# Decoder block on one core: softmax division in the output additions, biases of Wv on ScalarE, first Wo split on two engines, values of head pairs transposed together

## The reference, cut to what matters

```python
# B=4 batches, T=512 rows, C=512 columns
q = x @ Wq + bq;  k = x @ Wk + bk;  v = x @ Wv + bv     # 16 "heads" of 128, x layer-normed
att = softmax(q_T @ k / sqrt(128))                      # 128 x 128 per head: over the channels, not over the rows
x1 = x + (att @ v).reshape(...) @ Wo + bo
# cross attention of x1 (layer-normed) with ctx: 8 heads of 64 channels
x2 = x1 + gamma * softmax(q_h.T @ k_h / 8) @ v_h        # 512 x 512 per head and batch, v = k = ctx
# feed-forward with weights rounded to -s, 0, s
x3 = x2 + (silu(LN(x2) @ w1q.T) * (LN(x2) @ w3q.T)) @ w2q.T
```

## Time and profile before

| | before |
|---|---|
| time, median of 3 runs | 1224.45 us (1220.92 to 1225.1) |
| profiled execution, its own time | 1221.23 us |
| its span, first to last instruction | 1219.4 us |
| PE busy | 1144.5 us, 94% |
| DVE, ACT, POOL busy | 791.8 us (65%), 536.4 us (44%), 461.5 us (38%) |
| chain that ended last | PE 78%, DVE 11%, ACT 4%, POOL 2% |
| TensorE clock granted, mean | 0.983 of full speed |

### The profile page before, as it was taken

One profiled execution on the slowest core, in us unless ns is written; L12 is line 12 of the kernel. 1 busy time (PEld: TensorE's weight loads), 2 busy tenths in 40 slices (PEclk: granted clock), 3 DMA queues, 4 the chain that ended last, 5 costly groups with the idle time before them and its releaser, 6 DMA issues.

```text
span 1219.4 us, 16711 instructions
## 1 busy us (share of the span) xinstructions
PE 1144.5 (94%) x5856; PEld 952.4 (78%) x5856; DVE 791.8 (65%) x1469; ACT 536.4 (44%) x1129; POOL 461.5 (38%) x392
## 2 busy tenths in 40 slices
PE   4999988999999999899999978779999999999998
PEld 3888876878788888788888856568878887888786
DVE  7566559889465666453452378878867886787531
ACT  2455562314041244441232227657727762875230
POOL 2222249041341133461403026446625651674030
PEclk9999989999999999999999979979999999999999
DMA  6465553555302143312200132921103110310000
GB/s 224 131 186 181 185 173 109 180 175 170 110 19 85 59 156 113 127 55 70 69 1 1 35 129 66 323 70 54 52 21 102 51 35 34 94 46 1 35 1 35
DMA packets 50480, 114.76 MB, mean 94 GB/s; under 512 B 9721, under 2 KB 9721, under 8 KB 48362
## 3 DMA queue, kind: packets, MB, share of 16 engines
q1 hardware_dynamic: 50410, 113.84, 29.0%
HBM read 97.03 MB, written 16.79 MB: 93 GB/s over the span
## 4 chain that ended last, share of the span: by engine, by line
PE 78%; DVE 11%; ACT 4%; issue 3%; POOL 2%; DMA 1%; SPq 0%; POOLq 0%; ACTq 0%; DVEq 0%
PE bank L102 15%; PE bank L103 15%; PE bank L104 15%; PE bank L435 6%; PE bank L434 6%; PE bank L398 4%; PE bank L446 3%; PE bank L447 3%; PE bank L408 2%; PE bank L409 2%; PE bank L420 2%; PE bank L421 2%; POOL wal L1400 1%; DVE wlow L1352 1%; DVE wraw L1354 1%
## 5 line engine op out<-in xcount | busy, mean ns | idle before, releaser
L1063 ACT ACTIVATE yh<-bank 128x512 fp32r<-128x512 f32 x64 | 38.3, 598 | 244.4 <-PE bank L104 244.4
L434 PE MATMUL bank<-x3h,w 128*128 128x512 f32 (+1 forms) x352 | 141.4, 402 | 1.6 <-DVE x3l L678 1.6
L758 POOL TENSOR_SCALAR pe_x<-pe_x,xri,gam 128x512 f32<-128x512 f32 x128 | 100.9, 789 | 106.4 <-DVE xri L613 100.6
L435 PE MATMUL bank<-x3l,w 128*128 128x512 f32 (+1 forms) x352 | 138.9, 395 | 0.0
L1400 POOL TENSOR_TENSOR wal<-raw_a,wah 128x512 fp32r<-128x512 f32 x48 | 67.5, 1437 | 175.1 <-ACT wah L1084 175.1
L102 PE MATMUL bank<-yh,rh 128*128 128x512 f32 x256 | 101.5, 396 | 7.1 <-DVE xacc L1287 7.0
L1405 POOL TENSOR_TENSOR wbl<-raw_b,wbh 128x512 fp32r<-128x512 f32 x64 | 95.0, 1517 | 34.2 <-ACT wbh L1095 34.2
L102 PE MATMUL bank<-wah,ph 128*128 128x512 f32 x256 | 101.6, 397 | 6.6 <-POOL wal L1400 6.6
L609 DVE TENSOR_REDUCE xmx<-bank 128x1 f32<-128x512 f32 x128 | 87.4, 683 | 28.0 <-PE bank L409 26.8
L523 ACT ACTIVATE pe_x<-bank,xmx 128x512 f32<-128x512 f32 x128 | 87.9, 686 | 37.7 <-DVE xmx L609 36.3
L102 PE MATMUL bank<-wah,gh 128*128 128x512 f32 x256 | 101.0, 394 | 1.7 <-POOL wal L1400 0.8
(11 more groups left out here) (138 smaller groups left out, 2982.9 us busy)
## 6 DMA issues: line engine op xcount, KB each, us to landing
raw_a<-in_wk SPq DMA_DIRECT2D x8, 1024.0 KB, 5.2
raw_b<-in_wq SPq DMA_DIRECT2D x8, 1024.0 KB, 5.3
raw_a<-in_wo SPq DMA_DIRECT2D x8, 1024.0 KB, 5.8
raw_b<-in_wvt SPq DMA_DIRECT2D x8, 1024.0 KB, 4.8
x1d<-x_scratch SPq DMA_DIRECT2D x64, 128.0 KB, 2.7
kd<-in_ctx SPq DMA_DIRECT2D x64, 128.0 KB, 2.8
ternary_scratch<-wraw SPq DMA_DIRECT2D x24, 341.2 KB, 3.0
w<-ternary_scratch SPq DMA_DIRECT2D x2, 2730.0 KB
```

The lines of the kernel that those rows point to most:

```text
L434: pe.matmul(u_bank[w][0:m, :], lhs, x3h[:, c, :], start=c == 0, stop=False)
L435: mm = pe.matmul(u_bank[w][0:m, :], lhs, x3l[:, c, :], start=False, stop=c == CK - 1)
L758: pool.tensor_scalar(pe_x[:, q, :], pe_x[:, q, :], xri[:, q:q + 1], gam[:], ALU.mult, ALU.mult).then_inc(s["xpn"], 1)
```

## The change

Four edits are made together.

1. The exponentials are transposed undivided. `pe_t` waits for the exponentials (`s_read`), `dve_shares` makes one reciprocal of 128 x 8 sums for a group and keeps it (`rinv` has a place for each group), and `dve_out` multiplies by it while it adds: an operation with two tensors and one number per partition in place of an addition.
2. `dve_bias_v` only makes the four columns `dv`. ACT adds them to `raw_b` in four activations (`vadd`) ahead of its four copies in `act_split_b`. They stand behind ACT's wait for the last products that read `wbh`.
3. The first split of Wo (`step == GROUPS`) is shared as those of Wk are: DVE chunks 0 and 1, POOL chunks 2 and 3. `act_matrix(p, 0)` goes from the end of group 3's tiles into them (after the tiles of chunk 1).
4. The values of two heads are transposed together at `q == 0` of even heads, from a new tile `vd` (128 rows of ctx, one buffer, an added transfer of 256 KB for each pair of heads). ACT and DVE split a pair in one operation of 512 columns each. For odd heads SP no longer waits for a transpose. The tiles in `t_bank` are 40 in a turn, not 44.

```diff
@@ sp_head
             if h >= 2 or not isinstance(b, int) or b > 0:
                 sp.wait_ge(s["ql"], n - 1)
                 gate(sp, "sp")
-                sp.wait_ge(s["t_ready"], t_v(b, h - 2) + 1 if h >= 2 else t_v(b - 1, XH - 2 + h) + 1)
+            if h % 2 == 0:
+                if h or not isinstance(b, int) or b > 0:
+                    sp.wait_ge(s["t_ready"], t_v(b, h - 2) + 1 if h else t_v(b - 1, XH - 2) + 1)
+                sp.dma_start(vd[:], rows(ctx, b)[XD * h:XD * (h + 2), :]).then_inc(s["vd_in"], 16)
@@ pe_vt
-                mm = pe.transpose(tb[:, c * P:(c + 1) * P], kd[:, h % 2, c * P:(c + 1) * P], ident[:])
+                mm = pe.transpose(tb[:, c * P:(c + 1) * P], vd[:, c * P:(c + 1) * P], ident[:])
@@ pe_turn (act_turn and dve_turn alike)
-                        if q == 0:
+                        if q == 0 and h % 2 == 0:
                             pe_vt(pe, b, h)
@@ act_vt, dve_vt
+        def v_tile(h):
+            tb = t_bank[t_v(0, h) % 2][:].rearrange("p (c e n) -> p e c n", e=2, n=XD)
+            return tb, vts[:, h % 4:h % 4 + 2, :, 0:XD], vts[:, h % 4:h % 4 + 2, :, XD:P]
-            act.activation(vts[:, h % 4, :, 0:XD], tb[:, :, 0:XD], ACT.Copy).then_inc(s["vth"], 1)
+            act.activation(high, tb, ACT.Copy).then_inc(s["vth"], 1)
+            dve.tensor_tensor(low, tb, high.bitcast(F32), ALU.subtract).then_inc(s["t_free"], 1)
@@ pe_t
-                pe.wait_ge(s["pn"], n + 1)
+                pe.wait_ge(s["s_read"], n + 1)
@@ act_split_b
+            if step >= GROUPS:
+                act.wait_ge(s["dv"], GROUPS * p + step - GROUPS + 1)
+                for c in range(CK):
+                    act.activation(raw_b[:, c, :], raw_b[:, c, :], ACT.Identity, bias=dv[:, c:c + 1]).then_inc(s["vadd"], 1)
@@ act_scores
-                if g == GROUPS - 1:
-                    act_matrix(act, p, 0)
+                    if g == GROUPS - 1 and c == 1:
+                        act_matrix(act, p, 0)
@@ dve_bias_v
-            for h in range(HG):
-                dve.tensor_scalar(raw_b[:, h, :], raw_b[:, h, :], dv[:, h:h + 1], None, ALU.add).then_inc(s["wadd_b"], 1)
@@ dve_shares
-                dve.reciprocal(rinv[:, pr, :], rs[:, pr, :]).then_inc(s["rinv"], 1)
-                dve.tensor_tensor(w, w, rinv[:, pr, :].rearrange("p (a n) -> p a n", n=1).to_broadcast([P, 4, P]),
-                                  ALU.mult).then_inc(s["pn"], 1)
+            dve.reciprocal(rinv[:, g], rs[:, g]).then_inc(s["rinv"], 1)
@@ dve_scores
-                if g + 1 < GROUPS:
-                    dve_split_a(dve, p, g + 1)
+                dve_split_a(dve, p, g + 1)
                 dve_maxima(dve, p, g)
@@ dve_out
-            dve.tensor_tensor(xacc[:, i, a, :], xacc[:, i, a, :], late_bank(n)[:], ALU.add).then_inc(s["out_free"], 1)
+            dve.scalar_tensor_tensor(xacc[:, i, a, :], late_bank(n)[:], rinv[:, j, a // 2, q:q + 1], xacc[:, i, a, :],
+                                     ALU.mult, ALU.add).then_inc(s["out_free"], 1)
@@ pool_split_a
-            for c in range(2 if step < GROUPS else 0, CK):
+            for c in range(2 if step <= GROUPS else 0, CK):
```

More of the change, by code:

```diff
@@ L123, in decoder_block @@
             "wah", "wal_dve", "wal_pool", "wbh", "wbl",
-            "s_done", "s_read", "mx", "nmx", "rinv", "pn", "att_ready", "att_free", "pth", "ptl",
+            "s_done", "s_read", "mx", "nmx", "rinv", "dv", "vadd", "att_ready", "att_free", "pth", "ptl",
             "out_ready", "out_free", "xbo", "x1_ready", "x1_out",
@@ L145, in decoder_block @@
         dv = stack.enter_context(nc.sbuf_tensor("dv", [P, HG], F32))
-        mx, nmx, rs, rinv = (stack.enter_context(nc.sbuf_tensor(n, [P, 2, 4], F32)) for n in ("mx", "nmx", "rs", "rinv"))
+        mx, nmx = (stack.enter_context(nc.sbuf_tensor(n, [P, 2, 4], F32)) for n in ("mx", "nmx"))
+        rs, rinv = (stack.enter_context(nc.sbuf_tensor(n, [P, GROUPS, 2, 4], F32)) for n in ("rs", "rinv"))
         bank = [stack.enter_context(nc.psum_tensor(f"bank{i}", [P, 512], F32)) for i in range(8)]
@@ L217, in wal_dve @@
         def wal_dve(p, step):
-            return 2 * GROUPS * p + 2 * min(step, GROUPS)
+            return 2 * ((GROUPS + 1) * p + min(step, GROUPS + 1))
         def wal_pool(p, step):
-            return 6 * GROUPS * p + (2 * step if step <= GROUPS else 2 * GROUPS + 4 * (step - GROUPS))
+            return (6 * GROUPS - 2) * p + 2 * step + 2 * max(0, step - GROUPS - 1)
         def wadd_a(p, step):
@@ L226, in wadd_b @@
         def wadd_b(p, step):
-            return CK * load(p, step)
+            return CK * (GROUPS * p + step)
         def wait_a(eng, p, step, c):
-            if step < GROUPS and c < 2:
+            if step <= GROUPS and c < 2:
                 eng.wait_ge(s["wal_dve"], wal_dve(p, step) + c + 1)
-            elif step < GROUPS:
+            elif step <= GROUPS:
                 eng.wait_ge(s["wal_pool"], wal_pool(p, step) + c - 1)
@@ L509, in act_prep @@
             act.activation(qst[:, slot, :], x1d[:, slot, :], ACT.Copy).then_inc(s["qh"], 1)
+        def v_tile(h):
+            tb = t_bank[t_v(0, h) % 2][:].rearrange("p (c e n) -> p e c n", e=2, n=XD)
+            return tb, vts[:, h % 4:h % 4 + 2, :, 0:XD], vts[:, h % 4:h % 4 + 2, :, XD:P]
         def act_vt(act, b, h):
-            tb = t_bank[(5 * h - 4 if h else 0) % 2][:].rearrange("p (c n) -> p c n", n=P)
+            tb, high, low = v_tile(h)
             act.wait_ge(s["t_ready"], t_v(b, h) + 1)
-            act.activation(vts[:, h % 4, :, 0:XD], tb[:, :, 0:XD], ACT.Copy).then_inc(s["vth"], 1)
+            act.activation(high, tb, ACT.Copy).then_inc(s["vth"], 1)
         def act_px(act, b, h, q):
@@ L595, in dve_vt @@
         def dve_vt(dve, b, h):
-            tb = t_bank[(5 * h - 4 if h else 0) % 2][:].rearrange("p (c n) -> p c n", n=P)
-            dve.wait_ge(s["vth"], b * XH + (h + 1))
-            dve.tensor_tensor(vts[:, h % 4, :, XD:P], tb[:, :, XD:P], vts[:, h % 4, :, 0:XD].bitcast(F32),
-                              ALU.subtract).then_inc(s["t_free"], 1)
+            tb, high, low = v_tile(h)
+            dve.wait_ge(s["vth"], b * V_TILES + (h // 2 + 1))
+            dve.tensor_tensor(low, tb, high.bitcast(F32), ALU.subtract).then_inc(s["t_free"], 1)
         def dve_px(dve, b, h, q):
@@ L1108, in act_attention @@
                     e = act.activation(pw[:, pr, q * P:(q + 1) * P], pair_bank(pr)[:, q * P:(q + 1) * P], ACT.Exp,
-                                       bias=nmx[:, pr, q:q + 1], scale=SCALE_A, accum_out=rs[:, pr, q:q + 1])
+                                       bias=nmx[:, pr, q:q + 1], scale=SCALE_A, accum_out=rs[:, g, pr, q:q + 1])
                 e.then_inc(s["s_read"], 1)
@@ L1252, in dve_shares @@
         def dve_shares(dve, p, g):
-            for pr in range(2):
-                n = pair(p, g, pr)
-                dve.wait_ge(s["s_read"], n + 1)
-                dve.reciprocal(rinv[:, pr, :], rs[:, pr, :]).then_inc(s["rinv"], 1)
-                dve.wait_ge(s["rinv"], n + 1)
-                w = pw[:, pr, :].rearrange("p (a n) -> p a n", n=P)
-                dve.tensor_tensor(w, w, rinv[:, pr, :].rearrange("p (a n) -> p a n", n=1).to_broadcast([P, 4, P]),
-                                  ALU.mult).then_inc(s["pn"], 1)
+            dve.wait_ge(s["s_read"], pair(p, g, 1) + 1)
+            dve.reciprocal(rinv[:, g], rs[:, g]).then_inc(s["rinv"], 1)
         def dve_scores(dve, link, p):
@@ L1286, in dve_out @@
             dve.wait_ge(s["out_ready"], n + 1)
-            dve.tensor_tensor(xacc[:, i, a, :], xacc[:, i, a, :], late_bank(n)[:], ALU.add).then_inc(s["out_free"], 1)
+            if i == 0 and a == 0:
+                dve.wait_ge(s["rinv"], GROUPS * p + j + 1)
+            q = a % 2 * PB + i
+            dve.scalar_tensor_tensor(xacc[:, i, a, :], late_bank(n)[:], rinv[:, j, a // 2, q:q + 1], xacc[:, i, a, :],
+                                     ALU.mult, ALU.add).then_inc(s["out_free"], 1)
         def dve_between(dve, link, p, j, n):
```

30 lines of the change are left out of this document (18 added, 12 removed).

## The result

The changed kernel takes 1212.46 us in the median of five runs (1211.53 to 1214.28), the kernel before 1224.45 in five beside them: a ratio of 0.9915, 95% interval 0.9892 to 0.9937. By the two medians it is 12.0 us, by the ratio 10.4; the kernel before has medians of 1220.6 to 1222.2 in the later measurements, so 12.0 is at the high end. 21.0 us had been forecast. The median missed the range by half a microsecond; where the gain fell short of its sum is the matter of what follows.

What follows compares the result with a forecast made beforehand. PE bounds the kernel, waiting mainly for POOL's low parts and DVE's output additions; in turn 0 DVE sets the pace. 5.5 + 4.4 + 0 + 3.0 + 4.6 + 3.5 = 21.0 us gave 1202 us, range 1193 to 1212.

Steps and rivals of the forecast that it cites:

- First Wo split: Between scores and values: the twelve Wo products shorten to 3.86 us in pass 0, 2.9 in pass 1; gains 5.5 and 4.4.
- DVE's savings in pass 0: Values of pass 0: 32 additions leave DVE, so PE waits less for its output additions; 3.0 us gained, bounds 0 and 8.
- Biases on ACT: Between scores and values: ACT's additions delay wbh by 2.2 us, which just fits; 0 taken, at worst 2.2 us per pass.
- Value pairs in turns 1 to 3: Stage B, turns 1 to 3: PE saves 0.43 us per dropped transpose group, less longer turn starts; 4.6 us gained.
- Turn 0: Stage B's first turn: faster odd heads, x1 rows landing 3.5 us earlier at its end; 3.5 us gained, bounds 1 and 4.5.
- a clock that falls within the turn: Rival for turn 0: PE, less busy, drops to 1.2 GHz; 1227 us, no change; chance 0.04.

Runs made afterwards that it cites:

- experiment 2: Kernel before with only the first Wo split shared by DVE and POOL and the earlier pth; 1214.96 us, ratio 0.9938.
- experiment 1: Changed kernel with DVE's chain of small operations three slots later in group 0 of the first pass's values; 1205.14 us, ratio 0.9861.
- Experiment 10: Changed kernel with DVE's chain of small operations three slots later and Wv's bias additions back on DVE; 1200.25 us, ratio 0.9821.
- experiment 4: Changed kernel with the additions of Wv's biases back on DVE; 1207.91 us, ratio 0.9885.
- experiment 7: Changed kernel with the bias additions back on DVE and 32 one-column copies at the start of ACT's program; 1208.27 us, ratio 0.9893.
- experiment 11: Changed kernel with DVE's chain three slots later, bias additions back on DVE, and vd issued behind x1d and kd; 1201.38 us, ratio 0.9824.
- experiment 6: Changed kernel with 32 one-column memsets of an unused buffer at the start of DVE's program; 1208.68 us, ratio 0.9896.
- experiment 9: Kernel before with only DVE's chain of small operations three slots later; 1218.74 us, ratio 0.9977.

## Why the prediction missed

*First Wo split, 5.5 and 4.4 us: right.* In pass 0 the twelve products take 159.21 - 155.34 = 3.87 us (3.86 forecast), in pass 1 510.00 - 507.13 = 2.87 (2.9 forecast); PE of the changed kernel:

```profile
155.34 0.28 PE L104 MATMUL bank<-mh,wbl 128*128 128x256 f32 x1
...
158.40 0.50 PE L102 MATMUL bank<-wah,ph 128*128 128x512 f32 x1 [0.28 <-POOL wal L1415]
...
159.21 0.39 PE L102 MATMUL bank<-wah,ph 128*128 128x512 f32 x1
```

Both hold alone as well (experiment 2). The table gives the same, 5.5 and 4.4.

*DVE's savings in pass 0, 3.0 us gained: wrong, and this is the step that failed. Measured are 4.0 us lost, from 5.71 at 173.09 to 1.72 at 271.65, and PE's waits for `xacc` are 10.4 us where 3 to 5 had been forecast.* "PE arrives 5.5 us earlier, POOL doesn't, so their mutual blocking only moves." It moved onto the worst operations. I had counted blocking as if it depended on how long DVE's work is. It goes by the number of operations: a rounding of 1.1 us that meets POOL becomes 2.0, but a 0.17 us operation that meets a `wbl` becomes 1.2, and 14 of them stand in a chain. Through group 0 the kernel lost 5.1 us instead of gaining 0.7, with the clock at its lower level behind it. With the chain elsewhere the same stretch gains 3.7 us (experiment 1), but that does not confirm the term. It was counted from the 32 additions that leave DVE. Experiment 10 has them on DVE again and gains 4.1 us there (from 5.35 to 9.43, worked out like the table), and with the chain in its old place the stretch loses 4.0 us without them and 3.6 with them (experiment 4). So the runs show no gain from taking them off DVE, and that 3.7 lies near 3.0 is luck. The Trainium skill ("SBUF — State Buffer", section "Who interferes with whom") says that copies and `tensor_scalar` can take the pair that GpSimd uses, and that the later one is blocked for the whole of the other's instruction. The trace agrees: COPY and TENSOR_SCALAR of four columns take 1.0 to 1.2 us and end with POOL's operations, while the four BATCH_NORM_AGGREGATE beside POOL's `wal` keep to 0.82 together. The prediction used this rule for two `wal` and not for the chain that the same shift brought under `wbl`, though the row of 1.84 us for a 128 x 4 scaling already had this price.

*Biases on ACT, 0 us: 0.8 us too good in pass 1.* The additions have a pitch (start to start) of 0.61 us, four take 2.45 where 2.2 stood. The larger part is that the forecast compared 168.6 with 168.7 for pass 0 alone, with 3.9 us for the twelve products; for pass 1 it had 2.9 itself, so PE is there 1 us sooner. In pass 0 it just fits, as forecast; in pass 1 R waits for `wbl` (its first product came 0.60 us late by the trace's own idle time, 0.84 by the table; gone in experiments 2, 4, 7, 10 and 11):

```profile
511.47 2.58 ACT L1107 ACTIVATE raw_b<-raw_b,dv 128x512 f32<-128x512 f32 x4
513.92 2.21 ACT L1113 ACTIVATE wbh<-raw_b 128x512 fp32r<-128x512 f32 x4
```
```profile
519.79 0.36 PE L102 MATMUL bank<-pth,wbh 128*128 128x256 f32 x1 [0.60 <-issue]
```

Against DVE's version nothing is gained or lost by 725.28. Its larger price was the place of DVE's code.

*Value pairs in turns 1 to 3, 4.6 us: right, and hidden.* Without the stall, 1.4 us come from each of turns 2 and 3 (pairs alone: 5.25 to 8.03 over the two), where 4 x 0.43 - 0.2 = 1.5 stood. Turn 1 gives 1.1 us in that kernel. The changed kernel lost 1.8 us at one back edge, and by the first odd head of turn 2 (949.97 in before) the three kernels with the stall have fallen another 0.6 us behind the others that have the pairs: 2.4 in all, the length of the stall.

*Turn 0, 3.5 us: mechanism in part, sum not.* From 711.21 to 800.48 the changed kernel gains 0.7 us, the one with the pairs alone 3.0. The odd heads gain about 0.8 each (0.86 forecast), 2.4 us from 735.39 to 777.64. They are given back at both ends. At the beginning 2.0 us are lost, behind 1.1 gained. This belongs to the pairs: pairs alone loses 2.1 at the same place, Wo alone nothing. Part of it is that PE at 1.2 GHz lasts longer: windows of the changed kernel,

```profile
711.00:717.00 6.00, 3.33 (x7) 1.17 (x5) 5.35 (x11) 3.20 (x7) 3.32 (x3) 0.50 0.67 169
717.00:723.00 6.00, 2.98 (x8) 2.10 (x9) 5.08 (x25) 2.54 (x7) 1.54 (x2) 0.50 0.48 181
```

and of the kernel before:

```profile
711.00:717.00 6.00, 2.69 (x10) 1.98 (x9) 2.10 (x6) 0.63 (x1) 1.26 (x1) 0.78 0.44 175
717.00:723.00 6.00, 2.79 (x6) 0.91 (x5) 5.36 (x13) 3.35 (x8) 3.54 (x4) 0.78 0.58 168
723.00:729.00 6.00, 4.38 (x15) 3.34 (x16) 5.19 (x24) 2.60 (x9) 1.29 (x2) 0.50 0.45 179
```

In all, the clock record has 17.1 us at the lower level there against 13.7. With the memsets of experiment 6 it is 13.7 as well, and 1.5 us are still lost, so the clock is not the whole of it; the rest stays open. I had put 0.04 on a clock that falls within the turn; it falls only at its ends, but it shifts with them. At the end the x1 rows land 5.9 us earlier (785.40 against 791.29), of which 5.2 were gained before the turn began: 0.7 within the turn, where 3.5 had been forecast. PE is 6.7 us earlier, so DVE waits 2.31 us instead of 1.51. The added `vd` accounts for 0.6 of that. The end's low clock is 17.1 us against 13.7, and 10.2 with the memsets of experiment 6, where 0.5 us are gained from 777.64 to 800.48 and not 0.8 lost. Whether this part goes back to the code's place or only to when the idle time falls is open; no run separates them.

*Not in the sum at all: the stall at the back edge.* 1.8 us at once, 2.4 with what follows. Nothing in the diff or in the trace of before points at it, since the kernel before had its loop code well placed.

From after to the forecast by medians: 7.5 us for the chain (by the table), 1.8 for the stall, 0.8 for `wbl` in pass 1 make 10.1, and 1212.5 - 10.1 = 1202.4. Experiment 10, which has none of the three, is at 1202.5 us by its ratio beside the 1224.45 of the first measurement. The agreement is in part luck: the 7.5 us hold both more than the collision (experiment 9) and a gain that the forecast had counted for another reason.

## What to carry to other kernels

When an edit makes one engine earlier and leaves its neighbour where it was, list what the two do at the same time afterwards, operation by operation: long chains of tiny VectorE operations must not stand under a row of GpSimd operations, since each can wait for a whole one. Give such a chain a slot in which GpSimd is idle, ahead of nothing that TensorE waits for. And where a kernel has a loop, a change of some dozens of instructions far ahead of it can cost microseconds at the back edge: look for an idle "issue" behind it with instruction packets beside it, and compare with a padded copy before the difference is put down to the edit.
